# Loads of operands moved out of the first stage, and four max steps moved into it

## The reference

```python
x = x + attn(layernorm(x), Wq, Wk, Wv, Wo)
x = x + relu(layernorm(x) @ w1 + b1) @ w2 + b2

def attn(x):
    Q, K = rope(x @ Wq.T), rope(x @ Wk.T); V = x @ Wv.T      # per head
    scores = Q @ K.T / sqrt(16)
    scores = where(causal, scores, -inf)
    return (softmax(scores) @ V) @ Wo.T
```

## Time and profile before

| | |
|---|---|
| median of 3 runs | 2079.61 us (2079.06 to 2081.48) |
| profiled execution | 2078.35 us, span 2076.6 us |
| PE (TensorE) busy | 1935.3 us, 93% |
| DVE (VectorE) busy | 1861.4 us, 90% |
| ACT (ScalarE) busy | 1504.3 us, 72% |
| POOL (GpSimd) busy | 617.7 us, 30% |
| max reduces L840 | 768, 875.8 us, 1214 ns each |
| diagonal max L847 | 1024, 462.7 us, and 140.6 us for reading the accumulator |
| granted TensorE clock, mean | 0.979 |

### The profile page before, as it was taken

The page is one execution under the profiler, slowest core; times in us unless marked ns, Lnnn a source line. Parts: engine busy times, 40 slices in busy tenths (PEclk is TensorE's granted clock), DMA queues, the critical chain, the costliest instruction groups (busy, mean ns, idle before and its releaser), DMA issues. The chain is left out here.

```text
span 2076.6 us, 53487 instructions
## 1 busy us (share of the span) xinstructions
PE 1935.3 (93%) x19104; PEld 777.1 (37%) x19104; DVE 1861.4 (90%) x3959; ACT 1504.3 (72%) x3252; POOL 617.7 (30%) x1249
## 2 busy tenths in 40 slices
PE   5886599999999999999999999999999879999998
PEld 3443122232222323223233232332223246777776
DVE  7997899999999999999999999999999057777775
ACT  6995088888888898888988889888888823333332
POOL 7998521121221212212022120221212323333331
PEclk9999599999999999999999999999999989999999
DMA  5678231330313303033030321303210212222220
GB/s 188 232 246 231 94 70 31 63 69 18 71 33 69 69 18 70 25 78 63 23 70 23 80 46 41 70 23 80 42 35 19 73 59 86 86 87 81 81 86 26
DMA packets 133319, 153.17 MB, mean 74 GB/s; under 512 B 23904, under 2 KB 99424, under 8 KB 132832
## 3 DMA queue, kind: packets, MB, share of 16 engines
q1 hardware_dynamic: 133088, 150.19, 27.9%
HBM read 90.38 MB, written 59.77 MB: 72 GB/s over the span
## 5 line engine op out<-in xcount | busy, mean ns | idle before, releaser
L912 ACT ACTIVATE s_prob<-s_ps 128x512 f32<-128x512 f32 (+3 forms) x2560 | 1198.4, 536 | 179.7 <-PE s_ps L755 147.6
L840 DVE TENSOR_REDUCE s_part<-s_ps 128x2 f32<-128x1024 f32 x768 | 875.8, 1214 | 8.3 <-PE s_ps L738 7.4
L774 PE MATMUL s_ps<-s_prob,s_v 128*32 128x256 f32 (+3 forms) x10240 | 737.4, 360 | 14.3 <-ACT s_o L903 11.6
L738 PE MATMUL s_ps<-mk,mq 64*128 64x512 f16 (+3 forms) x2560 | 680.3, 357 | 56.5 <-DVE s_part L840 21.1
L755 PE MATMUL s_ps<-aq,ak 64*128 64x512 f16 (+3 forms) x2560 | 715.9, 351 | 4.5 <-ACT s_prob L912 1.5
L942 POOL TENSOR_SCALAR_AFFINE_SELECT s_prob<-s_prob 128x128 f32<-128x128 f32 x1024 | 286.1, 293 | 1093.3 <-ACT s_prob L912 1080.5
L847 DVE CUSTOM_DVE_ANT_0 s_ps<-s_ps,mask_sb 128x512 f32<-128x512 f32 (+3 forms) x1024 | 462.7, 525 | 4.0 <-PE s_ps L738 3.1
L774 PEld LDWEIGHTS s_ps<-s_prob,s_v 128*32 128x32 f32 x10240 | 201.9, 108 | 433.5 <-issue 214.8
L755 PEld LDWEIGHTS s_ps<-aq,ak 64*128 64x128 f16 x2560 | 177.0, 93 | 489.3 <-ACT s_prob L912 459.0
L738 PEld LDWEIGHTS s_ps<-mk,mq 64*128 64x128 f16 x2560 | 166.6, 93 | 129.4 <-DVE s_part L840 51.3
L1210 ACT ACTIVATE s_h_f<-s_ps,s_b_s 128x512 f32<-128x512 f32 x128 | 88.0, 687 | 105.7 <-PE s_ps L1075 84.8
(11 more groups left out here) (98 smaller groups left out, 1615.8 us busy)
## 6 DMA issues: line engine op xcount, KB each, us to landing
v_scratch<-s_vst SPq DMA_DIRECT2D x32, 512.0 KB, 4.0
s_v<-v_scratch SPq DMA_DIRECT2D x16, 1024.0 KB, 10.7
att_scratch<-s_o SPq DMA_DIRECT2D x64, 256.0 KB, 2.4
aq<-qk_scratch SPq DMA_DIRECT2D x96, 128.0 KB, 4.4
ak<-qk_scratch SPq DMA_DIRECT2D x96, 128.0 KB, 6.9
s_xin<-x SPq DMA_DIRECT2D x16, 512.0 KB, 4.3
qk_scratch<-s_r_lo SPq DMA_DIRECT2D x64, 128.0 KB, 2.3
qk_scratch<-s_r_hi SPq DMA_DIRECT2D x64, 128.0 KB, 2.4
```

What stands on the lines that cost most here:

```text
L738: nc.tensor.matmul(ps[:, bank_of(use + jj), 0:w], mq[rows, p, pair, qt * P:(qt + 1) * P], mk[rows, p, pair, kc * CH:kc * CH + w], start=Tr ...
L774: last = nc.tensor.matmul(ps[32 * j:32 * j + 32, O_BANK, cols], v[:, p, kb, j, :], prob[:, s % 2, j, cols], start=kb == 0 and part == 0, s ...
L840: nc.vector.tensor_reduce(part[:, qt // TPC, :, pair, qt % TPC, kc], ps[:, bank_of(use):bank_of(use) + 2, 0:w], AX.X, ALU.max).then_inc(m_ ...
L912: nc.scalar.activation(prob[:, s % 2, j, q0:CH], ps[:, s_bank(s, j), q0:CH], ACT.Exp, scale=1.0 / (SQK * DK ** 0.5)).then_inc(p_done, 1)
```

## The change

- In stage 1 SyncE loads only `mq`, `mk` of iteration 0 (8 DMAs). The other 8 and the 12 of `load_a` go to the start of stage 2, in this order: score operands, values, row store, row load, max operands of iteration 1, weights. The weights were second there.
- Max steps 0 to 3 (`EARLY = 4`) go to the end of stage 1: on TensorE behind the last value projection, on VectorE behind the last rotation. The four low halves of the last chunk stand behind the first of the four steps; two of them stood, and still stand for other chunks, at the end of the chunk's step.
- What both stages use (`max_pair`, `max_of_pair`, the maxima `part`, its semaphores) is moved out of stage 2; `part` is preset at the start of stage 1. GpSimd's and ScalarE's programs are the same.

```diff
+EARLY = 4
@@ stage 1, sync
                 if left == NC:
+
                     sp.wait_ge(ops_preset, 4)
-                    for i in range(2):
-                        sp.wait_ge(qk_out[i], 32 * (NC + 1))
-                        load_m(sp, ops, qk_d, i, i)
-                if left == NC - 1:
-                    load_a(sp, ops, qk_d, 0, 0)
+                    sp.wait_ge(qk_out[0], 32 * (NC + 1))
+                    load_m(sp, ops, qk_d, 0, 0)
@@ stage 1, tensor
             steps(step, pe)
+
+            pe.wait_ge(xlo_done, NCHUNK)
+            pe.wait_ge(rot_read, NG * NCHUNK + NM - KD)
+            for t in range(EARLY):
+                for pair in range(NP):
+                    max_pair(nc, pe, ops, ps, t, pair)
@@ stage 1, vector
-                split_rot(n, 0)
-                split_rot(n, 1)
+                if left > 1:
+                    split_rot(n, 0)
+                    split_rot(n, 1)
@@
             steps(step, dve)
-            for g in (2, 3):
-                split_rot(NCHUNK - 1, g)
+            dve.wait_ge(ops.const_in, 16)
+            dve.wait_ge(ops.part_preset, 1)
+            for t in range(EARLY):
+                for pair in range(NP):
+                    max_of_pair(nc, dve, ops, ps, t, pair)
+                if t == 0:
+                    for g in range(NG):
+                        split_rot(NCHUNK - 1, g)
@@ stage 2, sync
+            load_a(sp, ops, qk_d, 0, 0)
             load_v(0, 0)
+            store_rows(0, 0)
+            load_rows(0, 0)
+            load_m(sp, ops, qk_d, 1, 1)
             for dst, src in zip(w_f, weight_ds):
                 sp.dma_start(dst[:], src.rearrange("(k p) n -> p k n", p=P)).then_inc(w_in, 16)
-            store_rows(0, 0)
-            load_rows(0, 0)
             iteration(0, 0, first=True)
@@ stage 2, tensor
-            for t in range(LAG):
+            for t in range(EARLY, LAG):
@@ stage 2, vector
-                if t < STEPS_M:
+                if EARLY <= t < STEPS_M:
```

More of the change, by code:

```diff
@@ L153, in lo_outputs, with m_use, bank_of, crosses_diagonal @@
     nc.gpsimd.tensor_tensor(ops.att_lo[:, p], ops.o_in[:, p], ops.att_hi[:, p], ALU.subtract).then_inc(ops.att_lo_done, 1)
+M_BANK, NM = 0, 4
+STEPS_M = NIT * NS
+EARLY = 4
+def m_use(t, j):
+    return G * t + j
+def bank_of(use):
+    return M_BANK + use % NM
+def crosses_diagonal(qt, kc):
+    return kc == qt // TPC
+def max_pair(nc, pe, ops, ps, t, pair, heads=(0, 1)):
+    p, use = t // NS % 2, m_use(t, 2 * pair)
+    if pair == 0 and t % NS == 0:
+        pe.wait_ge(ops.m_in[p], 128 * (t // NS // 2 + 1))
+    qt, kc = MAX_TILES[t % NS]
+    w = min(CH, (qt + 1) * P - kc * CH)
+    for jj in heads:
+        rows = slice(HROWS * jj, HROWS * (jj + 1))
+        if crosses_diagonal(qt, kc):
+            pe.wait_ge(ops.m_read, use + jj + 1)
+        elif jj == heads[0]:
+            pe.wait_ge(ops.m_read, use + 2)
+        nc.tensor.matmul(ps[:, bank_of(use + jj), 0:w], ops.mq[rows, p, pair, qt * P:(qt + 1) * P],
+                         ops.mk[rows, p, pair, kc * CH:kc * CH + w], start=True, stop=True).then_inc(ops.m_ready, 1)
+def max_of_pair(nc, dve, ops, ps, t, pair):
+    qt, kc = MAX_TILES[t % NS]
+    use = m_use(t, 2 * pair)
+    w = min(CH, (qt + 1) * P - kc * CH)
+    if not crosses_diagonal(qt, kc):
+        dve.wait_ge(ops.m_ready, use + 2)
+        nc.vector.tensor_reduce(ops.part[:, qt // TPC, :, pair, qt % TPC, kc],
+                                ps[:, bank_of(use):bank_of(use) + 2, 0:w], AX.X, ALU.max).then_inc(ops.m_read, 2)
+        return
+    for jj in range(2):
+        bank = bank_of(use + jj)
+        dve.wait_ge(ops.m_ready, use + jj + 1)
+        dve.sem_inc(ops.masking, 1)
+        nc.vector.tensor_tensor_reduce(
+            out=ps[:, bank, 0:w], in0=ps[:, bank, 0:w], in1=ops.mask[:, CH - w:CH], scale=1.0,
+            scalar=MASKED, op0=ALU.add, op1=ALU.max,
+            accum_out=ops.part[:, qt // TPC, jj, pair, qt % TPC, kc:kc + 1]).then_inc(ops.m_read, 1)
 class Operands:
@@ L429, in _ @@
             nc.vector.memset(eps[:], EPS / SX ** 2).then_inc(eps_preset, 1)
+            dve.sem_inc(ops.m_read, NM)
+            nc.vector.memset(ops.part[:], -3e38).then_inc(ops.part_preset, 1)
             for n in range(2):
@@ L724, in _ @@
         def _(pe):
[L725 to L732, removed]
-                    rows = slice(HROWS * jj, HROWS * (jj + 1))
-                    if crosses_diagonal(qt, kc):
-                        pe.wait_ge(m_read, use + jj + 1)
-                    elif jj == heads[0]:
-                        pe.wait_ge(m_read, use + 2)
-                    nc.tensor.matmul(ps[:, bank_of(use + jj), 0:w], mq[rows, p, pair, qt * P:(qt + 1) * P],
-                                     mk[rows, p, pair, kc * CH:kc * CH + w], start=True, stop=True).then_inc(m_ready, 1)
             def filler_pair(p, s, pair):
@@ L832, in _ @@
         def _(dve):
-            def max_of_pair(t, pair):
-                qt, kc = MAX_TILES[t % NS]
-                use = m_use(t, 2 * pair)
-                w = min(CH, (qt + 1) * P - kc * CH)
-                if not crosses_diagonal(qt, kc):
-                    dve.wait_ge(m_ready, use + 2)
-                    nc.vector.tensor_reduce(part[:, qt // TPC, :, pair, qt % TPC, kc],
-                                            ps[:, bank_of(use):bank_of(use) + 2, 0:w], AX.X, ALU.max).then_inc(m_read, 2)
-                    return
-                for jj in range(2):
-                    bank = bank_of(use + jj)
-                    dve.wait_ge(m_ready, use + jj + 1)
-                    dve.sem_inc(masking, 1)
-                    nc.vector.tensor_tensor_reduce(
-                        out=ps[:, bank, 0:w], in0=ps[:, bank, 0:w], in1=mask[:, CH - w:CH], scale=1.0,
-                        scalar=MASKED, op0=ALU.add, op1=ALU.max,
-                        accum_out=part[:, qt // TPC, jj, pair, qt % TPC, kc:kc + 1]).then_inc(m_read, 1)
             def max_of_chunk(i, c):
```

39 lines of the change are left out of this document (15 added, 24 removed).

## The result

The changed kernel takes 2086.95 us (median of 13 runs, 2082.68 to 2089.92), the kernel before 2079.61 us beside it (13 runs, 2078.29 to 2083.73). The ratio of the comparison is 1.0021, 95% interval 1.0013 to 1.0030: 0.2% slower, 2.7 to 6.2 us. The two medians are 7.3 us apart, the two means 5.6. Forecast were +5.0 us and 2084.6. The profiled execution took 2089.34 us (span 2087.6), 11.0 us more than the one before.

A forecast was written before the change was run, and what follows sets the result against it. VectorE was taken to bound the kernel; the first value product moves to 206.4 + 59.6 = 266.0 against 260.30, +5.7 us, less 0.7 recovered: +5.0 us on 2079.61, so 2084.6 us, range 2079.5 to 2089.5.

The forecast's parts named there:

- High halves free of the store: End of stage 1: the last chunk's high halves on ScalarE no longer wait 10.86 us for a store, only for GpSimd.
- T = 206.4: T is SyncE's first issue of stage 2: 206.4 us instead of 212.81, a gain of 6.4 us.
- Cover of the twelve max operations: End of stage 1: VectorE's last 12 max operations, 4.6 us, run under the last stores, with 1.1 us to spare.
- The row store lands behind what is queued ahead: Start of stage 2: the row store lands about T + 17.5, after the queued loads; its reader issues at T + 18.
- rival 2: Start of stage 2: the row store lands early, ahead of queued loads; -3.3 us, 2081.3 us; chance 15%.
- GpSimd's start at T + 31.8, V at T + 59.6: Start of stage 2: late weights delay GpSimd's conversion and so V, TensorE's first value product; a new stall of 19.8 us.
- 0.7 us recovered: During the stall ScalarE and VectorE finish tiles they still had in hand at the first value product before: 0.7 us back.
- No clock cost: Start of stage 2: TensorE's clock is already low through the warm-up, so the stall takes no high clock away; 0 us.
- Rival 3: After the stall at stage 2's start: TensorE's clock stays low; +7 us, 2086.6 us; chance 12%.
- Everything after as before: The rest of the kernel after the first value product: no change in time.
- Rival 1: Start of stage 2: the stall is hidden, weights landing by T + 11.6; -14.1 us, 2065.5 us; chance 10%.
- Rival 4: Stage 1 ends no earlier than 208.5, max operations delaying low halves and outlasting the stores; +7 us, 2086.7 us; chance 10%.

The follow-up runs named there:

- e2: The kernel before with only the loads moved, the four max steps left in stage 2: 2086.36 us, ratio 1.0029 to before.
- e8: e1 with the preset of the partial maxima moved from VectorE's first instructions to just ahead of the early max steps: 2069.65 us, ratio 0.9951 to before.
- e5: The changed kernel with the weight loads third, behind score operands and values, ahead of the row store: 2078.28 us, ratio 0.9997 to before.
- e1: The changed kernel with the three weight loads put first, ahead of the score loads, at the start of stage 2: 2066.24 us, ratio 0.9933 to before.
- e4: The changed kernel with GpSimd converting one weight in each of iterations 0, 1 and 2, not at stage 2's start: 2075.58 us, ratio 0.9975 to before.
- e6: e1 with the last chunk's four low halves put ahead of all sixteen early max operations: 2066.16 us, ratio 0.9936 to before.
- e7: The kernel before with GpSimd converting one weight in each of the first three iterations, not at stage 2's start: 2091.55 us, ratio 1.0050 to before.
- e3: The changed kernel with all loads back where before has them, only the four max steps moved: 2072.33 us, ratio 0.9966 to before.

## Why the prediction was right

It forecast the mechanism and the sign, and the size of the stall. That the whole, +5.0 us, came as near as it did to the +7.3 of the medians is in part luck: the other terms missed by 1.6 to 5.0 us each, not all in one direction. Step by step:

- **High halves free of the store.** Right: all four wait for GpSimd. e2 has T at 206.81 for a forecast 206.2.
- **T = 206.4.** In the profiled execution of the changed kernel 211.41, 5.0 us off, the largest miss; by the prediction's own sign, a first load later than 208, the tail of stage 1 is the step that it had wrong. The last sine product starts at 197.06, where the same product had 193.52 in before: 3.5 us were lost earlier in stage 1, 1.1 before the first chunk's sine product, 1.0 in the gap of e8's table, the rest near 165 to 175 us, where TensorE's granted clock was 0.83. They do not follow from the change: e5, with the same stage 1, has T = 207.95. But e1 and e4, with the same stage 1 too, have 209.7, so a gain of 5 us in T is the best of four profiles and not the rule. Whether the change makes the lost microsecond of e8's table more frequent is open: five of the seven profiles with early steps have it, none of the three without. The remaining 1.5 us do belong to the change, as the way from the last shuffle to T is 13.5 us in the changed kernel, e1 and e5. The low halves end 7.1 us behind the shuffle's start (201.10 + 3.91 in the changed kernel) where 6.2 were summed; part of it is GpSimd's last sum, 1.72 us beside a low half of VectorE, 1.26 in the earlier trace rows. And the stores queue on SyncE, 6.4 us from the last low half to T, not 5.64. The sum gave both 0.2 us. The Trainium skill ("SBUF — State Buffer", section "SBUF: two separate sides") has such operations exclude each other; the trace agrees with the effect, 0.46 us on that operation, where the prediction had worked out 1.4 us as the worst.
- **Cover of the twelve max operations.** It holds, as T was later too: they end at 209.62, T is 211.41, and the issue of the value stores to T took 4.76 us, as before (208.05 to 212.81). e6 shows where it ends.
- **The row store lands behind what is queued ahead.** Right: its reader is issued at T + 18.5 (forecast T + 18), in e2 at T + 17.5. The Trainium skill ("DMA: Bandwidth & Descriptors", section "Queues, rings and completion order") says that completion is not first in, first out for one issuing engine, by which the small store could land ahead of the larger loads; no profile here shows that at this place, and rival 2 falls. What the prediction did not have is that 7.33 us of the wait are the issue of the store itself.
- **GpSimd's start at T + 31.8, V at T + 59.6.** T + 32.1 and T + 59.5. The stall, 19.8 us, is what e1 takes away.
- **0.7 us recovered.** Measured 0.76: from V to the first wide reduce 8.21 us in before, 7.45 here. Not foreseen were 1.5 us more up to M, the effect that e8 turned up.
- **No clock cost.** Right. The granted clock is low through the stall (0.50 in the stretch above) and rises about 274.8, 3.9 us behind V; in before, about 266.0, it rose 5.7 us behind it. Rival 3 falls, and with it, at this place, the rule of the Trainium skill ("TensorE: Matmul & The Clock Gate", section "HAM oscillation — how this bites in real kernels") that an idle wait costs a cold start: the clock was low already. Where it was high and TensorE ran dry, in e7, the trace agrees, 1.00 to 0.76.
- **Everything after as before.** M to the end took 465.4 us, not 462.8. The granted clock was 0.83 from 1620 to 1640 us (first line), 1.00 in before (second):

```profile
1620.00:1640.00 20.00, 18.41 (x171) 4.74 (x170) 2.75 (x5) 14.13 (x32) 4.50 (x16) 0.83 0.32 96
```

```profile
1620.00:1640.00 20.00, 19.19 (x195) 5.67 (x194) 0.00 (x0) 17.96 (x38) 3.98 (x8) 1.00 0.40 133
```

Counted from M, which comes 8.4 us later in the changed kernel, the drop stands too: 8 to 18 us behind M the granted clock is 0.66 in the changed kernel and 1.00 in before. e5 has the same drop and the same 465.4 us, and e6 is worse (470.6 us, in an execution 5.6 us over e6's median). But e2 and e7 are at 1.00 there and still take 465.4 and 465.8 us, where e1, e3 and e8 take 463.3 to 463.4. With one profile for each kernel the 2.6 us can't be told from noise, and the cause stays open; it is of the size by which the runs of one kernel differ.

So the 11.0 us between the two profiled executions are -1.4 (T) + 12.0 (T to V) - 2.3 (V to M) + 2.6 (tail), where the forecast had -6.4, +12.1, -0.7 and 0. The medians differ by less than the profiles, which fits parts of T and of the tail being noise, though that was not shown. Rival 1, 2065.5 us, was refuted for the changed kernel and is close to what e1 measured, 2066.24, once its condition (weights landed by T + 11.6) was made true. The closeness is partly luck: in the profiles T gave 3.1 us of its 6.4, T to V 7.8, and an unforeseen 2.0 came between V and M. Rival 4 needs an answer, since its time, 2086.7, is nearer to the median than the forecast, and its signs came out: T was later than 208.5 and VectorE's last max operation later than 206.2. Its mechanism is real but small: those operations ended 1.8 us before T, and all that is lost between the last shuffle and T is 1.5 us. It can't carry the loss either, since T is earlier than in before, and e1, with the same stage 1, is 20.7 us faster.

## What to carry to other kernels

A load that is moved out of a busy stretch does not stop costing; ask what is queued behind it at the new place and who starts only when that is there, here an engine with 26 us of work and 7 us of slack. When two changes relieve one place, find the third party that both wait for first: reordering three loads turned +7.3 us into -13.6 us. In these kernels the long GpSimd operations cost least where VectorE was waiting or in wide operations of its own, and most beside a short VectorE operation on which others wait. A conversion in the full steps that avoids the short operations was not tried.

## What the runs showed of the hardware

- A VectorE TENSOR_SCALAR on 32 columns in SBUF lasts 4.8 to 5.1 us instead of 0.18 when it meets GpSimd's 5.36 us TENSOR_SCALAR, and holds the operation behind it for 3 us. It ends when GpSimd's operation does, so its length is what is left of that: 2.81 us in e5, where it ends at 246.61 us and GpSimd's subtraction at 246.58; reduces of 1024 columns from PSUM beside the same conversion keep their 1.14 us each (24 in 27.37 us). In the changed kernel it happened inside the stall and cost nothing:

```profile
246.92 5.36 POOL L980 TENSOR_SCALAR s_w_f<-s_w_f 128x2048 f32<-128x2048 f32 x1
...
247.26 5.06 DVE L892 TENSOR_SCALAR s_nrow<-s_qmax_t 128x32 f16<-128x32 f32 x1
```

- The issue itself of a DMA right behind thirteen loads of the score and value operands took 7.2 to 7.7 us (changed, e4, e5), 4.0 when it came 3 us after them (e2), and behind the weights and the thirteen 10.4 to 12.0 us (e1, e6, e8), against 0.4 to 1.9 us with little ahead. SyncE is held for that long.
- A microsecond goes with which of two engines starts first, and 1.6 us over stage 2 with where an instruction stands ahead of a loop. Both are read from one profile of each kernel and are smaller than the spread of a kernel's runs (4.6 us over e1's five), so neither a median of five runs nor one profile settles a difference of 1 to 2 us between kernels.
